# A Perceiver layer on one core: key taps between the softplus steps, z projections moved behind the levels, and gate and up products in hi and lo parts

## The reference

```python
beta = jax.nn.sigmoid(b)
g = -jnp.exp(A_log) * jax.nn.softplus(a + dt_bias)
mixed = jax.nn.silu(causal_dwconv(mixed, conv_w))
core = gated_delta_rule(q, k, v, g, beta)
core = core * jax.lax.rsqrt(jnp.mean(core * core, -1, keepdims=True) + EPS) * gate_norm_w
core = core * jax.nn.silu(z.reshape(B, S, HV, DV))
h = resid + core.reshape(B, S, VAL_DIM) @ W_out
```

```python
gate_h = jnp.einsum('bsh,ehi->bsei', x, W_gate_e)
up_h = jnp.einsum('bsh,ehi->bsei', x, W_up_e)
exp_out = jnp.einsum('bsei,eih->bseh', jax.nn.silu(gate_h) * up_h, W_down_e)
moe_out = jnp.einsum('bseh,bse->bsh', exp_out, route)
```

## Time and profile before

| | us |
|---|---|
| median of 3 runs | 232.85 (232.74 to 232.89) |
| the profiled execution, its own time | 232.53 |
| its span in the trace | 230.6 |
| TensorE busy | 221.5 (96%) |
| ScalarE busy, VectorE busy | 143.9, 143.3 (62% each) |
| GpSimd busy | 122.2 (53%) |

### The profile page before, as it was taken

How to read it: one execution, slowest core, us unless ns; L and a number is a source line. 1 busy time by engine, 2 the same in 40 slices (tenths; PEclk the granted TensorE clock), 3 DMA queues, 4 the chain that set the end, 5 groups by cost and what they waited for, 6 DMA issues and landing times.

```text
span 230.6 us, 4195 instructions
## 1 busy us (share of the span) xinstructions
PE 221.5 (96%) x1559; PEld 194.0 (84%) x1559; DVE 143.3 (62%) x339; ACT 143.9 (62%) x264; POOL 122.2 (53%) x80
## 2 busy tenths in 40 slices
PE   8999999999999999889979999989999999999994
PEld 7757878888888888879969999864789999999993
DVE  2346666666666667356995776444334769887783
ACT  5257697777777775348776557545317848677570
POOL 1139878888888897732799910000000544555550
PEclk9999999999999999999999999999999999999999
DMA  6999999999999706999960000000000686960000
GB/s 200 393 430 415 416 420 418 415 418 416 414 419 417 293 3 229 424 423 421 418 283 0 4 0 3 0 0 0 1 3 0 203 345 239 411 259 7 0 0 23
DMA packets 8532, 52.94 MB, mean 230 GB/s; under 512 B 953, under 2 KB 1218, under 8 KB 6466
## 3 DMA queue, kind: packets, MB, share of 16 engines
q1 hardware_dynamic: 8514, 52.69, 56.9%
HBM read 52.56 MB, written 0.13 MB: 228 GB/s over the span
## 4 chain that ended last, share of the span: by engine, by line
PE 74%; DVE 9%; DMA 7%; ACT 4%; POOL 3%; issue 2%; ACTq 0%; DVEq 0%; POOLq 0%
PE psum L462 25%; PE psum L542 11%; PE psum L794 8%; DMA late_sb<-in_ctx_T 7%; PE psum L457 6%; PE psum L518 5%; PE psum L453 3%; PE psum L689 3%; PE psum L676 3%; POOL ctx_lo L375 2%; PE psum L718 2%; PE psum L745 1%; PE psum L560 1%; DVE work L1233 1%; DVE ring L1271 1%
## 5 line engine op out<-in xcount | busy, mean ns | idle before, releaser
L445 POOL TENSOR_TENSOR h_lo<-ring,h_hi 128x512 fp32r<-128x512 f32 x16 | 24.8, 1548 | 67.0 <-ACT h_hi L1061 61.0
L375 POOL TENSOR_TENSOR ctx_lo<-ring,ctx_hi 128x1792 fp32r<-128x1792 f32 x13 | 52.6, 4045 | 14.1 <-ACT ctx_hi L860 14.1
L462 PE MATMUL psum<-late_sb,work 128*128 128x448 f32 x68 | 27.8, 541 | 0.0
L462 PE MATMUL psum<-xT,late_sb 128*128 128x128 f32 x224 | 26.2, 276 | 0.1
L867 ACT ACTIVATE probsT_hi<-psum 128x512 fp32r<-128x512 f32 (+1 forms) x28 | 13.7, 540 | 19.3 <-PE psum L457 18.0
L462 PEld LDWEIGHTS psum<-xT,late_sb 128*128 128x128 f32 x224 | 25.5, 192 | 0.3 <-DVE xT L1377 0.3
L860 ACT ACTIVATE ctx_hi<-ring 128x1792 fp32r<-128x1792 f32 x13 | 22.1, 1701 | 3.4 <-DMA ring<-in_ctx 3.4
L1121 DVE TENSOR_REDUCE smalls<-psum 128x1 f32<-128x896 f32 x14 | 15.3, 1092 | 14.3 <-PE psum L518 9.1
L1145 DVE TENSOR_TENSOR probsT_lo<-psum,probsT_hi 128x512 fp32r<-128x512 f32 (+1 forms) x28 | 16.2, 619 | 7.3 <-ACT probsT_hi L867 7.1
L462 PEld LDWEIGHTS psum<-late_sb,work 128*128 128x128 f32 x68 | 11.9, 190 | 8.1 <-issue 7.8
L457 PE MATMUL psum<-early_sb,work 128*128 128x128 f32 x122 | 17.1, 274 | 0.3 <-ACT work L1016 0.3
(11 more groups left out here) (262 smaller groups left out, 493.5 us busy)
## 6 DMA issues: line engine op xcount, KB each, us to landing
late_sb<-in_ctx_T SPq DMA_DIRECT2D x14, 896.0 KB, 14.2
ring<-in_ctx SPq DMA_DIRECT2D x14, 896.0 KB, 13.2
late_sb<-in_late SPq DMA_DIRECT2D x10, 825.0 KB, 11.2
late_sb<-in_experts SPq DMA_DIRECT2D x8, 1024.0 KB, 9.9
late_slots<-in_experts SPq DMA_DIRECT2D x8, 1024.0 KB, 11.9
early_sb<-in_early SPq DMA_DIRECT2D x1, 512.0 KB, 3.6
early_sb<-in_early SPq DMA_DIRECT2D x1, 465.0 KB, 17.8
work<-in_levels SPq DMA_DIRECT2D x1, 416.0 KB, 19.1
```

The costliest lines, as they stand in the source:

```text
L375: nc.gpsimd.tensor_tensor(ctxNv[1][:, r % 2], ring[:, r], ctxNv[0][:, r % 2], ALU.subtract).then_inc(s["ctx_lo"], 1)
L445: nc.gpsimd.tensor_tensor(hT[1][:, e % 2, at, :], h32[:, at, :], hT[0][:, e % 2, at, :], ALU.subtract).then_inc(s["h_lo_done"], 1)
L462: last = nc.tensor.matmul(o, lhs(c), rhs(c), start=(c == 0), stop=(c == n - 1))
```

## The change

It has four parts.

Softplus and taps. The first four key taps (d = 1) are put between the steps of the second half of the softplus, and a factor is folded into `negA` so that one step goes. The keys' projections are signalled after two heads and after four. ScalarE evicts two key heads before the softplus's second exponential, and takes the tanh of the keys ahead of `decays(0)`, the squares ahead of `decays(1)`.

Work ahead of the levels and in them. The last two value heads take the place of z 0 and 1 ahead of the levels; z 0 to 3 go into the gaps of levels 2 to 5, none to the ends; z 4 to 7 follow the core's products, in place of six warm-up products.

Norm of the core. GpSimd's power of -0.5 takes the place of ScalarE's square root and VectorE's reciprocal. VectorE scales seven heads, ScalarE one. Head 0 of `project_out` goes ahead of the second transposes.

Gate and up. Weights and the normed x are split into hi and lo parts (`gate_up_hi` on ScalarE, `gate_up_lo` on GpSimd, four copies and four differences of 128x1024), and each product is three terms of two chunks. The parts of the weights lie in the memory of slots 2 and 3, so these are loaded after the fourth product (`gu_mm`). The silu table is loaded behind the square root of h, ahead of tanh. `gates` has two steps fewer behind the tanh, and the addition `xh` is moved behind it.

```diff
-Z_GAPS = {2: 2, 3: 3, 4: 5, 5: 7}
-Z_ENDS = {3: 4, 4: 6}
+Z_GAPS = {2: 0, 3: 1, 4: 2, 5: 3}
...
                 if j == W_SLOTS:
-                    sp.wait_ge(s["pv_done"], NG)
+                    sp.wait_ge(s["gu_mm"], 4)
...
+            def gate_up_lo(i):
+                w, b = GATE_UP[i]
+                pool.wait_ge(s["gu_hi"], i + 1)
+                nc.gpsimd.tensor_tensor(gate_up_parts[1][:, w, :, b, :], gate_up_32[:, w, :, b, :], gate_up_parts[0][:, w, :, b, :],
+                                        ALU.subtract).then_inc(s["gu_lo"], 1)
+
+            gate_up_lo(0)
+            for b in range(2):
+                pool.wait_ge(s["ms_done"], b + 1)
+                nc.gpsimd.tensor_tensor(s_("f", 4 * b, 4 * b + 4), s_("ms", 4 * b, 4 * b + 4), s_("marks", 7, 8).to_broadcast([P, 4]), ALU.pow)\
+                    .then_inc(s["f_done"], 1)
+            for i in range(1, 4):
+                gate_up_lo(i)
...
-            project(3)
+            project(3, range(0, 2))
...
-            project_z(0)
-            project_z(1)
+            project(3, range(2, 4))
...
-                if lv in Z_ENDS:
-                    project_z(Z_ENDS[lv])
...
-                pe.wait_ge(s["zs_done"], b + 1)
...
-            keep_warm(10)
+            for h in range(4, HV):
+                project_z(h)
+            keep_warm(4)
             def core_transposes(b):
                 pe.wait_ge(s["core_dve"], b + 1)
-                pe.wait_ge(s["core_act"], b + 1)
+                if b == 0:
+                    pe.wait_ge(s["core_act"], 1)
...
+            project_out(range(0, 1))
             core_transposes(1)
-            project_out(range(0, 4))
+            project_out(range(1, 4))
```

```diff
+            pe.wait_ge(s["x2_hi"], 2)
+
+            def gate_up(i):
+                w, b = GATE_UP[i]
+                pe.wait_ge(s["gu_hi"], i + 1)
+                terms = [(u, v, c) for u, v in ((0, 0), (0, 1), (1, 0)) for c in range(DC)]
+                for t, (u, v, c) in enumerate(terms):
+                    if t == DC:
+                        pe.wait_ge(s["gu_lo"], i + 1)
+                    if t == 2 * DC:
+                        pe.wait_ge(s["x2_lo"], 2)
+                    last = nc.tensor.matmul(bank[3 + 2 * w + b][:, :], half(x2_parts[u], c), gate_up_parts[v][:, w, c, b, :],
+                                            start=(t == 0), stop=(t == len(terms) - 1))
+                last.then_inc(s["gu_mm"], 1)
```

ScalarE's streams:

```diff
             for i in range(2):
-                act.wait_ge(s["proj_bank"], i + 1)
                 for k in range(4):
+                    act.wait_ge(s["proj_bank"], 1 + k // 2 if i == 0 else 3)
                     n = 4 * CHANNELS[i] + k
-                    last = nc.scalar.activation(qkvT[:, n, :], bank[1 + i][:, k * P:(k + 1) * P], ACT.Copy, scale=conv_w[:, n, 3:4])
+                    last = nc.scalar.activation(qkvT[:, n, :], raw_at(i, k), ACT.Copy, scale=conv_w[:, n, 3:4])
+                    if (i, k) == (0, 1):
+                        last.then_inc(s["tap0_done"], 1)
+                        act.wait_ge(s["ln1p_first"], 1)
+                        nc.scalar.activation(s_("f"), s_("ms"), ACT.Exp).then_inc(s["ln1p_exp"], 1)
...
-            decays(0)
             act.wait_ge(s["conv_done"], 1)
             nc.scalar.activation(bank[5][:, :].rearrange("p (k t) -> p k t", k=HK), qkvT[:, HK:2 * HK, :], ACT.Tanh, scale=0.5).then_inc(s["tanh_kb"], 1)
-            decays(1)
+            decays(0)
             act.wait_ge(s["k_done"], 1)
             square(0, 1)
+            decays(1)
...
+            def gate_up_hi(i):
+                w, b = GATE_UP[i]
+                if i == 0:
+                    act.wait_ge(s["late2_in"], 16 * (LATE_PARTS - FIRST_PARTS))
+                nc.scalar.activation(gate_up_parts[0][:, w, :, b, :], gate_up_32[:, w, :, b, :], ACT.Copy).then_inc(s["gu_hi"], 1)
...
-            silu_z(0)
             copy_xt(5)
             silu_v(1)
-            silu_z(1)
+            silu_z(0)
+            gate_up_hi(0)
             copy_xt(6)
             keep_columns(6)
-            nc.scalar.activation(s_("spare", 0, 1), s_("eps", 3, 4), ACT.Sqrt).then_inc(s["act_chain"], 1)
-            chain[0] += 1
+            gate_up_hi(1)
...
+            silu_z(1)
+            act.wait_ge(s["zo_done"], 1)
+            act.wait_ge(s["f_done"], 1)
+            nc.scalar.activation(core[:, 3, :], core[:, 3, :], ACT.Copy, scale=s_("f", 3, 4)).then_inc(s["core_act"], 1)
             for b in range(2):
                 act.wait_ge(s["core_T"], b + 1)
                 nc.scalar.activation(coreT[:, 4 * b:4 * b + 4, :], bank[3 + b][:, :].rearrange("p (h t) -> p h t", h=4), ACT.Copy,
                                      scale=early_at("gate_norm")).then_inc(s["coreT_done"], 1)
+                if b == 0:
+                    gate_up_hi(2)
+            nc.scalar.activation(s_("spare", 0, 1), s_("eps", 3, 4), ACT.Sqrt).then_inc(s["act_chain"], 1)
+            chain[0] += 1
+            gate_up_hi(3)
             act.wait_ge(s["h_done"], 1)
...
             nc.scalar.activation(half(xT, 1), bank[2][:, 0:P], ACT.Copy, scale=s_("w2p", 1, 2)).then_inc(s["x2_copied"], 1)
+            nc.scalar.activation(half(x2_parts[0], 1), bank[2][:, 0:P], ACT.Copy, scale=s_("w2p", 1, 2)).then_inc(s["x2_hi"], 1)
             link(nc.scalar.activation(scratch[:, :], hh[:, :], ACT.Square, accum_out=s_("sd", 0, 1)))
             nc.scalar.activation(s_("sd", 1, 2), s_("sd", 0, 1), ACT.Sqrt, scale=1.0 / D, bias=s_("eps", 2, 3)).then_inc(s["hsd_done"], 1)
+            nc.scalar.activation(s_("spare", 0, 1), s_("eps", 3, 4), ACT.Silu).then_inc(s["act_chain"], 1)
```

VectorE's streams:

```diff
+        def raw_at(i, k):
+
+            o = bank[1 + i]
+            if i == 0 and k >= 2:
+                o = bank[6]
+            at = k % 2 if i == 0 else k
+            return o[:, at * P:(at + 1) * P]
...
+            def tap(i, d, k):
+
+                n = 4 * CHANNELS[i] + k
+                return V.scalar_tensor_tensor(qkvT[:, n, d:T], raw_at(i, k)[:, 0:P - d], conv_w[:, n, 3 - d:4 - d],
+                                              qkvT[:, n, d:T], ALU.mult, ALU.add)
...
+            V.tensor_tensor(s_("n2"), s_("sp"), s_("f"), ALU.add).then_inc(s["dve_chain"], 1)
+            V.tensor_tensor(s_("kap"), s_("sp"), s_("f"), ALU.subtract).then_inc(s["dve_chain"], 1)
+            chain[0] += 2
+            dve.wait_ge(s["tap0_done"], 1)
+            tap(0, 1, 0).then_inc(s["dve_chain"], 1)
+            dve.wait_ge(s["dve_chain"], chain[0])
+            V.reciprocal(s_("n2"), s_("n2")).then_inc(s["dve_chain"], 1)
+            V.tensor_tensor(s_("kap"), s_("kap"), s_("negA"), ALU.mult).then_inc(s["dve_chain"], 1)
+            chain[0] += 3
+            dve.wait_ge(s["tap0_done"], 1)
+            tap(0, 1, 1).then_inc(s["dve_chain"], 1)
+            dve.wait_ge(s["dve_chain"], chain[0])
+            V.tensor_tensor(s_("kap"), s_("kap"), s_("n2"), ALU.mult).then_inc(s["dve_chain"], 1)
+            chain[0] += 2
+            dve.wait_ge(s["tap0_done"], 2)
+            tap(0, 1, 2).then_inc(s["dve_chain"], 1)
+            dve.wait_ge(s["dve_chain"], chain[0])
+            V.tensor_tensor(s_("g"), s_("kap"), s_("au"), ALU.add).then_inc(s["rates_done"], 1)
+            dve.wait_ge(s["tap0_done"], 2)
+            tap(0, 1, 3).then_inc(s["dve_chain"], 1)
             chain[0] += 2
             dve.wait_ge(s["dve_chain"], chain[0])
...
-            taps(0, (1, 2, 3))
```

```diff
+            mean_squares(0)
+            gate_output(0)
+            mean_squares(1)
+            normalize(0, range(0, 3))
+            gate_output(1)
+            normalize(1, range(4, HV))
...
+            V.tensor_scalar(half(x2_parts[0], 0), bank[1][:, 0:P], s_("w2p", 0, 1), None, ALU.mult).then_inc(s["x2_hi"], 1)
+            dve.wait_ge(s["x2_hi"], 2)
+            for c in range(DC):
+                V.scalar_tensor_tensor(half(x2_parts[1], c), bank[1 + c][:, 0:P], s_("w2p", c, c + 1), half(x2_parts[0], c),
+                                       ALU.mult, ALU.subtract).then_inc(s["x2_lo"], 1)
...
+                V.tensor_scalar(s_("e1"), early_at("iota"), s_("idf", 0, 1), weight, ALU.is_equal, ALU.mult).then_inc(s["dve_chain"], 1)
+                V.tensor_scalar(s_("e2"), early_at("iota"), s_("idf", 1, 2), weight, ALU.is_equal, ALU.mult).then_inc(s["dve_chain"], 1)
+                chain[0] += 2
+                dve.wait_ge(s["dve_chain"], chain[0])
+                V.tensor_tensor(s_("lg"), s_("e1"), s_("e2"), ALU.subtract).then_inc(s["dve_chain"], 1)
+                V.tensor_tensor(s_("top"), s_("e1"), s_("e2"), ALU.add).then_inc(s["dve_chain"], 1)
+                chain[0] += 2
+                dve.wait_ge(s["dve_chain"], chain[0])
                 dve.wait_ge(s["tanh_done"], turn)
-                link(V.tensor_scalar(s_("w", 0, 1), s_("th"), 0.5, 0.5, ALU.mult, ALU.add))
-                link(V.tensor_scalar(s_("w", 1, 2), s_("th"), -0.5, 0.5, ALU.mult, ALU.add))
```

(5 more changed lines are left out.)

143 lines of the change are left out of this document (65 added, 78 removed).

## The result

The changed kernel is slower: 235.28 us, median of 4 runs (235.09 to 235.8), beside 232.8 us for the kernel before in the same comparison; the ratio is 1.0093, 95% interval 1.0066 to 1.0119. The forecast was 231.2. The profiled execution took 235.8 us, its span is 234.0.

A forecast was written before the change was run, and what follows sets the result against it. TensorE was last waited for in 74% of the span, with different bounds in the four stages touched. The terms -0.4 - 0.5 + 0.3 - 1.05 = -1.65 us gave 231.2 us as median, range 230.3 to 232.5.

The forecast's parts named there:

- rival 5: Norm of the core: GpSimd's second lo part holds VectorE's last four heads; +0.55 us, 233.4 us; chance 0.08.
- Step A: Softplus and key taps, start of the levels: the key convolution ends earlier, the level start gains 0.4 us.
- Step B: Levels: two z projections leave level ends (0.90 us), less VectorE's wait and ScalarE's lateness; net gain 0.5 us.
- Step C: Norm of the core: GpSimd's power, later transposes, 14 project_out instructions left instead of 16; a loss of 0.3 us.
- Step D: Gate and up in parts, shorter route, silu's table loaded earlier: down products come sooner, gain taken as 1.05 us.
- The moved loads: Two experts' weights wait for the fourth gate/up product, about 160 us; no cost, some 8 us of cover.
- Rivals 1 to 4: Larger gain, 230.5 (0.10); late hi copies, 232.2 (0.10); VectorE holds levels and start, 232.1 (0.08); little change, 232.55 (0.12).

The follow-up runs named there:

- the ruler: The kernel before plus VectorE instructions on unused tiles, some alone, five beside a GpSimd subtraction of 512 columns; its total time says nothing.
- e1: The changed kernel with one more wait: GpSimd's lo parts 1 to 3 begin only when VectorE has scaled the last heads; 230.44 us, ratio 0.9898.
- e11: The changed kernel itself run once more, unaltered; 234.84 us, ratio 1.0094.
- e6: The changed kernel without hi and lo parts of gate and up, products in f32 as before the change; 231.41 us, ratio 0.9915.
- e2: The changed kernel with all eight heads scaled and gated on VectorE from PSUM, GpSimd's order untouched; 231.71 us, ratio 0.9949.
- e5: The changed kernel with GpSimd's second lo part moved ahead of its two root instructions, no new wait; 230.49 us, ratio 0.9866.
- e7: The changed kernel with each lo part cut into four subtractions of 256 columns; 231.91 us, ratio 0.9942.
- e9: The kernel before plus two dead GpSimd subtractions of 1024 columns, back to back, at the second half's mean squares; 236.27 us, ratio 1.0171.
- e10: The kernel before plus one dead GpSimd subtraction of 2048 columns at the second half's mean squares; 236.3 us, ratio 1.0143.
- e3: The changed kernel with 12 more warm-up products on TensorE between head 0 of project_out and the second transposes; 234.34 us, ratio 1.0067.

## Why the prediction was wrong

**The step that failed is the dismissal of rival 5, and its price.** The mechanism was named with the right instruction, the right half of the heads and about the right time (second lo part at 145.48, forecast 146.5), and given 0.08. What I held against it was a reading of rows: 256 columns in 0.41 us and two of 128 in 0.48 were "no sign of a doubled rate". They could not decide it. In the ruler 256 columns take 0.35 us and 128 take 0.28, so such short ones are nearly all fixed cost; what decides is the step from 512 to 1024 columns, or one step measured both from SBUF and from PSUM, and the trace of before has no such pair for this instruction. The Trainium skill (SBUF — State Buffer, Who interferes with whom) states what then happened beside the subtractions (beside the power on 4 columns it did not happen), and the text gave it a sentence and too small a chance. The second reason, "they read one SBUF tile, whereas the held ones read two", took one way into the hold for the only one: in the ruler both were held (0.75 and 0.81 us).

**The price was short too.** Rival 5 had one lo part in the way and moved the second transposes by 2.2 us. By its own rows that was even too much: four heads behind 149.05 end at 150.0, and the transposes stood at 148.2, so 1.8. But there were two lo parts: the third hi copy was ready at 147.86 (L998, 146.81 + 1.05), so GpSimd went on without a gap, and the next head was caught again. The norm lost 5.15 us where 0.3 was forecast. 0.24 is the new relay, by e1. Of the other 4.91, 3.20 is the hold: in e11, where the clock kept its 1.0, the norm takes 15.35 us (138.78 to 154.13) beside 12.15 in e1. The remaining 1.71 is the clock in after's profiled execution (4.87 beside 3.19 us for the 14 rows is 1.68). The fall of the clock was in no step and no rival.

**Step A, the level start**: 0.56 us for 0.4. **Step B, the levels**: 0.67 for 0.5. The two z projections gave their 0.90. Level 5 then took 3.05 us on the chain (132.39 to 135.44) beside 2.80 before (133.33 to 136.13): 0.25, where I read 0.2 for VectorE's updates. The lateness of ScalarE that I put at 0.15 to 0.2 was not there. Its copy of level 6 starts at 136.62, just behind the hi copy's end at 136.57, and that is 0.43 us after the transposes' start (136.19), beside 0.42 before (136.89 to 137.31). **Step C without the hold**: 0.24 for 0.3. **Step D**: 1.05 for 1.05; e6 splits it into 0.86 and 0.17. The load in front of silu was gone, and its switch took 1.28 us where one was left (L1077). **The moved loads** cost nothing: from the first down products to the end of the span it is 69.44 us before and after. Rivals 1 to 4 did not happen: the levels kept 0.67 and not 0.9, the hi copies added 0.01, and the start and the route gained what they were to gain.

Without the hold the sum is -2.02 us in e1's profile (-0.57 - 0.65 + 0.24 - 1.04), and its timed median is 2.2 us below that of before (ratio 0.9898), of which 0.1 lies outside of the span. So the change is worth some 2 us, and GpSimd's order took it and 2.5 more. Shown by runs: the hold (e1, e2, e5, e6, e7, e9, e10). Shown in part: the clock, which e3 keeps up. Its fall costs 1.6 to 1.7 us in the profiled executions that have it (after, e9, e10), and between timed runs only 0.4 to 1.3. Open: the last 0.6 us between e1 and e2, of which 0.36 lies outside of the span, and why two executions with the same 2.99 us of idle time differ in the clock.
